# POOL waits for a group's landing ahead of every second group of gathers, in a graph and mixture layer on one core

## The reference, cut to what matters

```python
xn = layernorm(x)                       # 6250 nodes, 256 channels
# graph attention over 200000 edges, 4 heads of 64
Wh  = xn @ W
e   = leaky_relu(Wh_i . a_src + Wh_j . a_dst)      # i = src, j = dst of the edge
e   = exp(e - max(e))
h   = segment_sum(Wh[dst] * e, src) / segment_sum(e, src) + Wh
gnn = relu(layernorm(h) @ ffn_w + ffn_b)
# a second branch: second-order linear attention, 8 heads of 32, over the same xn
x   = x + gnn + mix(xn)
# top 2 of 8 experts, each 256 -> 512 -> 256 with gelu
x   = x + moe(layernorm(x))
```

## Time and profile before

| what | value |
|---|---|
| median of 3 runs | 4567.11 us |
| span of the profiled execution | 4552.4 us (14.7 us under that median) |
| PE busy | 3118.0 us, 68% |
| DVE busy | 2760.2 us, 61% |
| ACT busy | 1951.9 us, 43% |
| POOL busy | 2159.7 us, 47% |
| gathers, L884 | 1564, 962 ns each, 1504.4 us busy, 1594.4 us idle before them |
| weigh, L1565 | 440, 1214 ns each |
| products of the second branch, L1582 | 392, 1218 ns each |
| all DMA | 452.92 MB, 99 GB/s over the span |

### The profile page before, as it was taken

The page is one execution under the profiler, slowest core; times in us unless marked ns, Lnnn a source line. Parts: engine busy times, 40 slices in busy tenths (PEclk is TensorE's granted clock), DMA queues, the critical chain, the costliest instruction groups (busy, mean ns, idle before and its releaser), DMA issues.

```text
span 4552.4 us, 80191 instructions
## 1 busy us (share of the span) xinstructions
PE 3118.0 (68%) x17657; PEld 2176.0 (48%) x17657; DVE 2760.2 (61%) x6376; ACT 1951.9 (43%) x5742; POOL 2159.7 (47%) x2438
## 2 busy tenths in 40 slices
PE   4888266666666666667777777777776444777895
PEld 2333133333333333456555555555555333666785
DVE  8999866666666666656555555565555465434322
ACT  4777133333333333344444444444444222544674
POOL 5877455455555555544444444444444532123123
PEclk8888677777887877788888888888888776988998
DMA  2222244343434434433333333333333333334344
GB/s 67 99 96 89 89 103 103 106 103 101 110 100 104 121 99 105 110 89 90 84 92 81 87 89 83 83 87 85 84 88 83 94 112 130 105 109 150 96 136 134
DMA packets 326431, 452.92 MB, mean 99 GB/s; under 512 B 79020, under 2 KB 261482, under 8 KB 326052
## 3 DMA queue, kind: packets, MB, share of 16 engines
q0 software_dynamic: 85552, 236.37, 19.0%
q1 hardware_dynamic: 217896, 194.32, 14.9%
q10 hardware_dynamic: 22860, 20.83, 1.6%
HBM read 366.49 MB, written 84.82 MB: 99 GB/s over the span
## 4 chain that ended last, share of the span: by engine, by line
PE 27%; DVE 21%; issue 20%; another core or an unknown queue 15%; DVEq 7%; ACT 5%; POOL 3%; ACTq 1%; DMA 1%; SPq 1%; POOLq 0%
PE bank L2046 8%; PE bank L2230 4%; PE bank L2242 4%; DVE room L1582 3%; PE bank L2080 3%; DVE room L1374 2%; DVEq L1541 2%; PE bank L2091 2%; DVE room L1373 2%; DVE room L1565 2%; DVE room L1535 1%; DVE room L1555 1%; PE bank L2055 1%; ACT room L1175 1%
## 5 line engine op out<-in xcount | busy, mean ns | idle before, releaser
L884 POOL DMA_INDIRECT room<-table,room x1564 | 1504.4, 962 | 1594.4 <-DVE room L1565 1127.9
L2046 PE MATMUL bank<-room 128*128 128x260 f32 x3520 | 1053.1, 449 | 472.4 <-DVE room L1565 291.2
L2046 PEld LDWEIGHTS bank<-room 128*128 128x128 f32 x3520 | 752.3, 225 | 634.4 <-issue 510.2
L1565 DVE TENSOR_TENSOR room<-room,bank 128x1024 f32<-128x1024 f32 x440 | 534.3, 1214 | 71.3 <-issue 41.1
L1582 DVE TENSOR_TENSOR room<-bank,room 128x1024 f32<-128x1024 f32 x392 | 477.5, 1218 | 162.6 <-remote 88.9
L1175 ACT ACTIVATE room<-bank 128x512 f32<-128x512 f32 (+1 forms) x588 | 252.4, 487 | 393.0 <-remote 306.0
L1555 DVE TENSOR_REDUCE room<-bank 128x32 f32<-128x128 f32 x440 | 125.2, 285 | 426.9 <-remote 263.8
L1107 ACT ACTIVATE bank<-room 128x16 f32<-128x16 f32 x440 | 80.8, 184 | 671.8 <-DVE room L1559 432.9
L1100 ACT ACTIVATE spare<-away,ones 128x512 bf16<-128x512 bf16 x440 | 317.6, 722 | 57.3 <-ACT away L1097 7.6
L2080 PE MATMUL bank<-ident,room 128*128 128x128 f32 x1764 | 298.8, 325 | 22.3 <-issue 11.1
L1115 ACT ACTIVATE bank<-room 128x96 f32<-128x96 f32 x392 | 96.4, 246 | 506.5 <-DVE room L1585 331.5
(11 more groups left out here) (321 smaller groups left out, 5010.7 us busy)
## 6 DMA issues: line engine op xcount, KB each, us to landing
spare<-rows_dram SPq DMA_DIRECT2D x440, 128.0 KB
room<-table,room POOLq DMA_INDIRECT x1564
kv_dram<-room SPq DMA_DIRECT2D x49, 324.0 KB, 2.2
room<-kv_dram SPq DMA_DIRECT2D x196, 81.0 KB
y_dram<-planes SPq DMA_DIRECT2D x119, 128.0 KB
room<-xs_dram ACTq DMA_DIRECT2D x110, 128.0 KB
q_dram<-room SPq DMA_DIRECT2D x49, 192.0 KB, 1.9
room<-q_dram SPq DMA_DIRECT2D x196, 48.0 KB
```

The source lines that it names most:

```text
L884: pool.indirect_dma_start(G[:, k.slot, u, :], None, table, bass.IndirectOffsetOnAxis(ap=ixbuf[:, k.slot, u:u + 1].bitcast(I32), axis=0)).t ...
L1565: dve.tensor_tensor(Gw[:, h, :, 0:C].rearrange("p u (h d) -> p u h d", h=GH), G[:, bass.ds(slot, 1), :, 0:C].rearrange("p a u (h d) -> p ( ...
L2046: ins = pe.matmul(pbank[1 + h][:, 0:TW], OH[:, s, u, :], Gw[:, h, u, :], start=(u == 0), stop=(u == U - 1))
```

## The change

For groups in even slots (0 and 2) the report of the group before now stands ahead of the first gather; for odd slots (1 and 3) it stays ahead of the fourth.

```diff
--- before.py
+++ after.py
@@ -880,11 +880,13 @@
             if k.after(4):
                 pool.wait_ge(gw_done, free)
             alone(pool, idx_ready, k.n + 1)
+            if k.slot % 2 == 0 and k.after(1):
+                report(k + -1)
             for u in range(U):
                 pool.indirect_dma_start(G[:, k.slot, u, :], None, table,
                                         bass.IndirectOffsetOnAxis(ap=ixbuf[:, k.slot, u:u + 1].bitcast(I32), axis=0)
                                         ).then_inc(gathered[k.slot], 16)
-                if u == 2 and k.after(1):
+                if u == 2 and k.slot % 2 == 1:
                     report(k + -1)
 
         def report(k):
```

## The result

The change takes 4314.18 us (median of 4 runs, 4304.35 to 4323.19) against 4561.09 us before (4 runs, 4539.55 to 4596.7): ratio 0.9446, 95% interval 0.9401 to 0.9492. It is 5.5% faster; the forecast said 4496 us, 1.6%, and 4314 us lies under its range.

What follows compares the result with a forecast made beforehand. The edge loop was held bound by DVE pausing for code delayed by gathers, not by arithmetic. 4552.4 - 144 + 73 = 4481 us, plus 14.7 us to the median, gave 4496 us, 1.6% faster; range 4385 to 4640.

Steps and rivals of the forecast that it cites:

- The lengthened pauses: Edge loop: 57 DVE pauses end later behind shifted gather bursts, adding 73 us, 66 of it before 1990 us.
- my bounds: Limits on DVE's pause terms in the edge loop: 0 to 73 us lengthened, 0 to 287 us shortened.
- The pauses as missing code: Edge loop: DVE's pauses over 2 us, 171 with 855.7 us, read as waiting for code delayed by gathers.
- the 8.30 us of the earlier trace: Example DVE pause from about 695 to 703.41 us, ending 2.26 us after the last gather's end.
- The shortened pauses: Edge loop: 61 DVE pauses span new holes, with 287 us behind them; half taken, 144 us saved.
- The price of the moved wait: POOL ahead of even groups: 119 waits up to 1.98 us, 166 us in full, counted as 0 through idle time.
- The rule on taking turns: DMA engines alternate queues packet by packet, so fetches share with gathers and the sum would be near zero.
- a rival of no change: Edge loop: holes too short to help, shifts matched by savings; 4567 us, give or take 40, chance 0.22.
- All holes work, nothing comes back: Edge loop: every hole ends its DVE pause, saving all 287 us; 4353 us, chance 0.17.
- The slower rival: Laps before 1990 us: bursts shift and holes don't help; 4640 us, or 4733 if waits are uncovered, chance 0.16.
- its dearer price: Slower case with POOL's waits no longer covered by idle time: 4567 + 166 = 4733 us.
- The signs to look for: Profile after: some 120 DMA waits on POOL, 150 to 200 us; DVE pauses about 785 us, fewer over 8 us.

Runs made afterwards that it cites:

- e4: Kernel before without the edge loop's 1564 gathers, POOL raising the semaphores itself: 3505.41 us, ratio 0.7789 at the 4500 level.
- e1: Kernel before plus a wait for the landing ahead of every second group, reports left as before: 4279.02 us against 4502.66, ratio 0.950.
- e16: Repeat of e1, the hole without the sooner report, against the kernel before: 4277.43 us, ratio 0.9485 at the 4500 level.
- e2: The change, but with the report ahead of the first gather of every group: 4462.57 us, 0.9912 of the kernel before.
- e18: The change, but with holes ahead of every group in laps 46 to 89: 4204.71 us against 4580.13 for the kernel before, ratio 0.9184.
- e9: The change itself run again, at the 3505 level: 3825.31 us against 3507.17 for the kernel before, ratio 1.0913.
- e6: The change, but with the early report in slot 0 only, one hole in four groups: 3598.19 us, 1.027 of the kernel before, 3505 level.
- e13: The change once more, without the larger written-out program in its company: 3831.84 us against 3504.67 for the kernel before, ratio 1.0934.
- e5: Kernel before with each gather fetching 4 floats a row instead of 260: 3480.12 us against 3504.41, ratio 0.9932, 3505 level.
- e12: Repeat of e5, gathers of 4 floats a row instead of 260, against the kernel before: ratio 0.9932, 3505 level.
- e3: Kernel before with four POOL memsets ahead of each even group from the second lap on, no wait for landing: 4376.52 us, ratio 0.9719.

## Why the prediction was wrong

The direction and the place held, and so did the core of the mechanism: e4 shows that the gathers cause DVE's pauses, e1 that the hole and not the report makes the gain. What failed is one term of the sum; beside it, what the pauses consist of was read wrongly, which the sum did not use.

- **The lengthened pauses, +73 us: the step that failed.** I took 73 us "since the ends follow the bursts", 66 of it beside the keys, and expected +29 us there. It came to -173 us. In the table the rest of the sum is off by 31 us together; this stage alone is off by 202 us. I had kept the pauses where they were in the trace and moved the bursts' ends. But the pauses do not stay. The 49 pauses beside the keys that stand behind a shifted place took 190 us before; ahead of the same 49 instructions DVE idles 31 us with the change. New pauses over 2 us stand ahead of 22 other instructions there, 64 us. In all, pauses over 2 us beside the keys went from 74 with 315 us to 36 with 104 us, and the longest is 4.2 us. No choice within my bounds reaches this: with nothing lengthened and all of the 74 us saved, the stage comes to -74 us, 99 us short. The missing part is pauses to which the sum gave no saving. I read it as one backlog: what comes through in one hole need not be waited for behind the next, and with a hole at least once in two groups there is hardly a burst long enough to wait for. The counts show that the pauses go, not why.
- **The pauses as missing code.** I had read "remote" as DVE waiting for its own code, with no partner, and took the 8.30 us of the earlier trace rows for an example. But their partner is PE, and the record is against my reading for the larger part of the pauses: 95 of the 171 pauses, 561 of 855 us, end with a late rise of a semaphore that PE raises. 46 pauses, 182 us, have no releaser at all, and DVE's stream creeps; for these code is possible and not shown. So "time in which an engine had its data and did not run" does not hold for the remote part. The sum hung only on pauses ending behind bursts, which most of them do.
- **The shortened pauses, half of 287 us.** Beside the keys more than the whole 74 us was saved. Beside the queries it was less than the half, -40 us (-23 in e16) where I had -74: an odd group right behind a wait for DVE has no hole ahead of it, and e2 and e18 show that more holes gain another 109 to 131 us there (107 for e2 against e1, in one set).
- **The price of the moved wait, 0.** About right at this level: DVE waits 14.0 us for the report instead of 1.5. POOL's waits came out of its idle time as said. But the cover came from the pauses themselves. Where they are absent, the same wait costs 318 us (e9: 3825.31 - 3507.17), nearly twice the 166 us that I had named as the full price, and there each of the 195 even groups starts 2.5 us or more behind the gather before it, where I had 119 groups and 1.98 us.
- **The rule on taking turns.** By the Trainium skill ("DMA: Bandwidth & Descriptors", section "Queues, rings and completion order") each DMA engine goes round its queues packet by packet. I had made of it a rival of no change, and the measured 0.9446 rules that out. How full the DMA engines are does not decide either: at the 4500 level the pauses stand beside a DMA share of 0.50, at the 3505 level there is no remote one with more bytes a second moved (126 GB/s over e6's span, 99 before). How long one turn takes no run here shows.
- **The rivals.** "All holes work, nothing comes back" gave 4353 us and had 0.17; it was the nearest, and too slow still by 39 us, with the same +73 in it. Its premise did not hold, since 69 us came back as short gaps; that errors of both signs bring it near is luck. The slower rival does not describe this level. At the 3505 level the change is slower, but by DVE's wait for the report, its dearer price, and not by pauses that end a hole later.
- **The signs to look for.** I had asked for 120 DMA waits of 150 to 200 us (155 of 410.0), pauses of 785 us (551.1), and fewer over 8 us (15 pauses over 8 us before, none after). "About 2 us" for the gaps ahead of even groups was too short: the smallest is 2.51 us, the median 2.84. "DVE <- POOLq" rose to 14.0 us, short of the tens that would have made the report a bound.

**Open.** What the level hangs on. It is not the company of a kernel (e13, e18), and not the chip: both levels came on the same one. It reaches beyond the gathers of the loop: what follows the loop takes 826 to 840 us in every profile at the 4500 level and 760 to 769 us in every one at the 3505 level. Open too is what is held back. It delays PE's semaphores or its products, it makes the streams of DVE, PE and SP creep, and it ends for all three at once (703.3 to 703.5 us); late code, late signals and a slow way that all of them share may each look like this, and no run tells them apart. Whether the bytes or the number of row requests block it was asked by e5 and e12, neither at the level that could answer.

## What to carry to other kernels

When engines pause with no releaser that the profile knows, look at which semaphore rises when the pause ends, whether other engines go on at the same time, and what POOL issues then; try a hole in that before anything on the paused engine. Weigh a hole by the stage: it pays where steps are long and the issuing engine has slots to spare, and costs time where the issuing engine then becomes the bound. And measure the kernel before in more than one set of runs: a change that cures a stall is worth nothing, or less, where the stall does not occur.

## What the runs showed of the hardware

- The same kernel took 4480 to 4597 us in four sets of runs and 3499 to 3510 us in three, at one level within a set.
- At the 4500 level, 1564 gathers of 128 rows of 1040 bytes cost 997 us over leaving them out (4502.66 against 3505.41); TensorE's granted clock over steps 0 to 207 was 0.78 with them and 0.99 without.
- At the 4500 level, with the gathers, 894 of 1813 recorded rises of PE's semaphores in the loop came over 1 us behind the recorded end of the matmul that raised them; without the gathers none of 2012 did, nor any of 1990 at the 3505 level with them (e6).
- The landing of the last gather is seen by POOL 1.98 us after its end. A gather of POOL that waits for the landing of the group before started 2.51 us or more after that group's end, in the median 2.84 us with the change and 2.66 us in e9.
- A memset of 128 x 512 floats on POOL took 0.52 us (776 in e3, 0.514 to 0.538 us).
